# Row-max jobs in key-chunk order, and six of eight head groups in a hardware loop

## The reference

```
mod = silu(condition) @ Wada + bada          # 6 vectors: shift, scale, gate, twice
xm  = layernorm(x) * (1 + sc_a) + sh_a
q, k, v = xm @ Wqkv                          # 16 heads of 32
attn = softmax(causal(q @ k.T / sqrt(32)))
x   = x + gt_a * ((attn @ v) @ Wproj + bproj)
xm  = layernorm(x) * (1 + sc_m) + sh_m
x   = x + gt_m * (gelu(xm @ W1 + b1) @ W2 + b2)
```

## Time and profile before

| | |
|---|---|
| median of 3 runs | 2236.31 us (2230.17 to 2239.51) |
| the profiled execution's own time | 2236.31 us |
| its span | 2234.1 us |
| attention phase | 346 to 1391 us, and 8 us of its end |
| POOL busy in 346 to 1391 us | 861.07 us |
| DVE busy in it | 743.77 us |
| ACT busy in it | 631.35 us |

### The profile page before, as it was taken

How to read it: one execution, slowest core, us unless ns; L and a number is a source line. 1 busy time by engine, 2 the same in 40 slices (tenths; PEclk the granted TensorE clock), 3 DMA queues, 4 the chain that set the end, 5 groups by cost and what they waited for, 6 DMA issues and landing times. The chain is left out here.

```text
span 2234.1 us, 31272 instructions
## 1 busy us (share of the span) xinstructions
PE 2154.2 (96%) x11326; PEld 1443.9 (65%) x11326; DVE 1286.7 (58%) x2872; ACT 929.2 (42%) x1780; POOL 965.7 (43%) x380
## 2 busy tenths in 40 slices
PE   6999999999999999999999999899999999999998
PEld 5888885454444545454444544677888888888886
DVE  4778876777777777777777754784313213133132
ACT  2111115566566656655655665335322222222221
POOL 2001007979799797988979773760000000000000
PEclk9999999999999999999999999999999999999999
DMA  6548346235261522625243222784101011011010
GB/s 235 206 151 266 127 168 158 63 76 120 54 138 46 119 66 63 149 49 131 52 112 80 59 77 63 247 319 155 67 37 57 0 56 56 0 56 56 0 38 19
DMA packets 129240, 222.96 MB, mean 100 GB/s; under 512 B 8526, under 2 KB 26006, under 8 KB 128920
## 3 DMA queue, kind: packets, MB, share of 16 engines
q1 hardware_dynamic: 107992, 179.38, 29.5%
q10 hardware_dynamic: 21120, 41.95, 5.1%
HBM read 146.31 MB, written 74.98 MB: 99 GB/s over the span
## 5 line engine op out<-in xcount | busy, mean ns | idle before, releaser
L1170 ACT ACTIVATE prob<-st 128x512 f32<-128x512 f32 (+3 forms) x1280 | 608.0, 542 | 387.2 <-PE st L1344 371.6
L1140 POOL TENSOR_TENSOR psum_k<-psum_k,prob 128x2048 f32<-128x2048 f32 (+1 forms) x150 | 670.8, 4472 | 21.0 <-ACT prob L1170 5.4
L1226 DVE TENSOR_REDUCE part<-mx 128x1 f32<-128x512 f32 x702 | 459.0, 685 | 107.0 <-PE mx L1324 104.0
L1344 PE MATMUL st<-q_st,k_st 98*128 98x512 f32 (+3 forms) x1280 | 489.8, 395 | 8.1 <-ACT prob L1170 4.1
L1324 PE MATMUL mx<-k_st,qx_st 96*128 96x512 f32 (+3 forms) x1189 | 465.7, 407 | 17.7 <-DVE part L1222 5.6
L1738 DVE TENSOR_TENSOR m_g_lo<-m_g,m_g_hi 128x512 fp32r<-128x512 f32 x128 | 88.6, 693 | 494.8 <-ACT m_g_hi L1652 494.8
L1344 PEld LDWEIGHTS st<-q_st,k_st 98*128 98x128 f32 x1280 | 242.7, 190 | 194.3 <-issue 103.1
L1324 PEld LDWEIGHTS mx<-k_st,qx_st 96*128 96x128 f32 x1189 | 224.0, 190 | 169.7 <-DVE part L1226 107.3
L1222 DVE CUSTOM_DVE_ANT_0 unused<-mx,mask_row 128x256 bf16<-128x256 f32 x487 | 230.6, 485 | 124.8 <-PE mx L1324 119.7
L1361 PE MATMUL o_ps<-prob,v_sb 128*32 128x512 f32 (+3 forms) x2560 | 285.6, 551 | 3.0 <-POOL prob L1123 3.0
L1648 ACT ACTIVATE m_g<-m_hid,vcol 128x512 f32<-128x512 f32 x128 | 88.2, 689 | 480.3 <-PE m_hid L1835 480.3
(11 more groups left out here) (168 smaller groups left out, 2593.5 us busy)
## 6 DMA issues: line engine op xcount, KB each, us to landing
k_st<-qk_scratch SPq DMA_DIRECT2D x96, 256.0 KB, 8.3
qx_st<-qk_scratch SPq DMA_DIRECT2D x96, 256.0 KB, 5.0
q_st<-qk_scratch SPq DMA_DIRECT2D x96, 256.0 KB
qk_scratch<-st_hi ACTq DMA_DIRECT2D x16, 1024.0 KB, 4.2
qk_scratch<-st_lo ACTq DMA_DIRECT2D x16, 1024.0 KB, 6.9
xs<-in_x_dram SPq DMA_DIRECT2D x8, 1024.0 KB, 8.7
v_sb<-v_scratch SPq DMA_DIRECT2D x8, 1024.0 KB, 15.4
o_scratch<-o_sb SPq DMA_DIRECT2D x32, 256.0 KB, 2.3
```

Of the source, the lines that this page charges most:

```text
L1140: nc.gpsimd.tensor_tensor(dst, src, prob[:, s % BUF, :, m:], ALU.add).then_inc(pool_added, 1)
L1170: nc.scalar.activation(prob[:, s % BUF, h, m:], st[n % RING][:, m:], ACT.Exp, scale=SCALE).then_inc(exp_done, 1)
L1226: nc.vector.tensor_reduce(most, bank[:, 0:w], AX.X, ALU.max).then_inc(mx_free, 1)
L1344: nc.tensor.matmul(st[n % RING][:, m:], k_st[u][0:MROWS, h, kt * P:(kt + 1) * P], q_st[0:MROWS, pos % 2, h, m:], start=True, stop=True).th ...
```

## The change

Three edits, of which the third has the most instructions:

```
-                       for h in range(GH) for t in range(TT) for kc in range(c + 1)[::-1]]
+                       for kc in range(c + 1)[::-1] for h in range(GH) for t in range(TT)]
...
-            work.insert(start + LATER, (pos or QC) - 1)
+            work.insert(start + (LATER if pos else 0), (pos or QC) - 1)
...
-        rest = [it for it in self.items[len(self.tail):self.items.index(QC - 1) + 1]
-                if not self.norm(it) and (isinstance(it, int) or it[0])]
+        rest = [it for it in self.items[len(self.tail):self.items.index(QC - 1) + 1] if not self.norm(it)]
...
-            for g in range(NG):
-                body(g, g % 2, g > 0, g < NG - 1)
+            body(0, 0, False, True)
+            with eng.Fori(0, NG // 2 - 1) as i:
+                body(2 * i + 1, 1, True, True)
+                body(2 * i + 2, 0, True, True)
+            body(NG - 1, 1, True, False)
```

## The result

The changed kernel took 2259.93 us (median of 4 runs, 2256.48 to 2262.04) against 2236.32 us (4 runs). The ratio is 1.0113, 95% interval 1.0095 to 1.0132: about 1% slower. I had forecast 2241 us with a range of 2224 to 2264. The profiled execution of after took 2256.66 us, its span is 2254.9 us, 20.8 longer than before.

A forecast was written before the change was run, and what follows sets the result against it. Bound taken: POOL's additions in a chain POOL, ACT, POOL, with DVE nearly as close. Sum: 2236.31 + 2.8 (order) + 3.7 (clock) + 2.8 (turn) + 0.6 - 6.6 - 2 + 4 = 2241.6, rounded to 2241 us; range 2224 to 2264.

The forecast's parts named there:

- the slower rival: Whole kernel: jumps back stall PE, ACT and DVE, with turn delay and clock falls, giving 2261 us; chance 0.23.
- the account that I took as mine: Whole kernel: the forecast itself, 2241 us with its own range 2232 to 2250; chance 0.42.
- The jump back, 2 us, twice: At the loop's round end: PE idle 2 us each time, bounds 0.86 and 4.3 us; +4 us in all.
- PE has products queued at that place: At the loop's round end: queued matmuls on PE as the reason to take 2 us a jump, below 4.3.
- The waits in the loop, -8.6 us: Groups in the loop: POOL's pauses 0.1 us shorter each, -6.6 us; ACT's first exponentials gain too, -2 us.
- the bound of 0.9: First half of a loop group (pos 0): POOL's shorter pauses save no more than some 0.9 us.
- Registers at 0: Loop body in attention: 710 register instructions a round on PE and 462 on ACT, taken to cost 0 us.
- The order of the jobs, +2.8 us: Reordered blocks: changes up to block 13 hidden, +0.4 us in blocks 16 and 17, over 7 groups.
- The early turn, +0.4 us a group: Block 8, groups 0 to 6: last `st` waits for `mcol`, delaying POOL's addition; bounds 0 and 0.8; +2.8 us.
- The clock, +3.7 us: Block 17, now nearly all short jobs: two more falls to half clock; bounds 0 and 11 us.
- the sign I had set for myself: Groups 1 to 6 without a jump changing over 2 us each would mean registers or waits weigh more than given.
- Phase a, +0.6 us: Phase a: one job more, group 0's share growing from 29 to 30 items, one DVE operation of 0.6 us.

The follow-up runs named there:

- edits 1 to 3 alone: New job order and early turn of batch 3 against the kernel before, all groups written out without the hardware loop: 2249.32 us, ratio 1.0059.
- the loop alone: Hardware loop put on the old job order, against the kernel before: 2245.56 us, ratio 1.0046.
- Keys alone: Jobs ordered by key chunk instead of by head, against the kernel before; turn of batch 3 as before, no loop: 2241.72 us, ratio 1.0023.
- the turn alone: Turn of batch 3 moved early, against the kernel before; jobs by head as before, no loop: 2250.46 us, ratio 1.0076.
- the test with a delay: Last exponential of block 8 cut into four pieces in every group, against the kernel before: 2238.13 us, ratio 0.9994.
- the kernel that differs in group 0 alone: Four exponentials of step 17 cut into four pieces each, in group 0 only, against the kernel before: 2238.57 us, ratio 1.0003.

## Why the prediction was right or wrong

The result lies in the range, 19 us above the value. The range holds it thanks to the slower rival, to which I gave 0.23; the account that I took as mine would have left it out (2232 to 2250). Most of the miss, 15 of 19 us, is in the loop. My terms for it were -6.6, -2 and +4, so -4.6 us; alone it cost 0.46%, 10 us. The other terms together were +9.9 us; edits 1 to 3 alone cost 0.59%, 13 us, so 3 more.

- **The jump back, 2 us, twice: the step that failed.** It cost 4.38 and 4.30 us of PE's time, my upper bound (4.3), and the clock at half in the next block, which I had only in the rival. In the loop alone that is 5.8 and 6.2 us against before, 12 in all, 8 more than taken; in after the two blocks are 4.9 us longer each time, 9.7 in all. "PE has products queued at that place" hid nothing: the last of them start at 755.90 us and take 0.40, and PE stands still behind them. That a taken jump stops PE was right; the overlap was wrong, and the size was that of the slower rival.
- **The waits in the loop, -8.6 us.** POOL's pause shrank to 0.08 us, not 0.05, and a first part without a jump gained 0.6 us. That is the 9 pauses times 0.07 us: from POOL's first addition to the end of its last one of pos 0 it takes 52.0 to 52.1 us in the groups of the loop without a jump, and 52.6 before. All of it came through, so the bound of 0.9 that I had set never came into play. Pos 1 and ACT gave 0.2 us a group at most (the second parts of groups 2, 3 and 5 of the loop alone are 76.0 to 76.1 us, against 76.2 to 76.4 before, all behind a fall in block 7). For the two groups with a jump the gain is inside the price of the jump. So some 2.5 to 3.5 us, 5 to 6 fewer than taken.
- **Registers at 0: right.** Groups of the loop without a jump are shorter than before.
- **The order of the jobs, +2.8 us.** Keys alone cost 0.23%, 5 us. That POOL hides what blocks 2 to 6 gain in length was right, to 0.1 us. Wrong was "Are diagonal jobs in a row dearer than singly? ... so no": I compared with block 7, whose `st` are short. Under full `st`, 11 jobs in a block are dearer than their sum (block 10 +0.4, where I had -0.25; block 4 +0.5, where I had +0.15). Block 8, where I had nothing, grew by 0.5, and block 17 by 0.45 instead of 0.3. Blocks 2 and 13 came as computed (-0.2, -0.3), the latter though I had POOL letting nothing of it through.
- **The early turn, +0.4 us a group.** The mechanism was right, and in the turn alone POOL's idle time of 1.46 us is the 1.4 forecast; in after itself it is 2.3 to 3.8 us, and no run takes that apart. But I followed only the `st` behind the turn; the products wait too, and block 8 grew by 0.7, close to my bound of 0.8: +2 us.
- **The clock, +3.7 us.** Block 17 fell in seven groups, five more than before, and is 8.8 us longer over them. But the short jobs by themselves, as I had argued, don't do it: keys alone fell there in two groups, like before, and the turn alone in six with the old jobs. And the sign I had set for myself, groups without a jump over 2 us longer, did come in three of the four (group 4: 135.40 against 131.1; group 1 only 1.2), but did not mean what I had tied to it, registers or waits: the loop alone has first parts 0.6 us shorter there. It was the falls, the turn and the order.
- **Phase a, +0.6 us:** not seen; attention began at 345.0 us, against 346.8.

The rival "the loop's cost lies on the path" had 12 us for the jumps, 5.6 for the turn, 11 for falls, -4 for the waits. Measured: 12 in the loop alone and 9.7 in after, about 5, about 9 in block 17 of after, -2.5 to -3.5. It had no term for the order of the jobs, which cost 5 us alone, so that it came so near to 2260 is in part luck. But it was the better account, in its parts as well. The Trainium skill's rule on taken branches ("Runtime: NRT & Kernel Launch", Instruction fetch mechanics) spoke for it, and I underrated that. My own value rested on a cover, queued products, that I had not looked for in the rows at a group's end.

What stays open: what makes the clock fall in block 17 of one group and not of the next. That a turn with a wait in block 8 costs more than its own length is shown over the runs (0.32 and 0.76%, of which its own length explains some 0.1 and 0.2), and that the clock is lower with it too (0.982 and 0.979, against 0.985), but not by what path; the test with a delay was too small to tell. And that what stops PE at the jump is the fetch of its instructions is inferred: the packets are there, the wait for them is in no row.

## What to carry to other kernels

A jump back over a long body must be priced as PE standing still plus the half clock behind it, unless the trace shows work queued there; multiply by the taken jumps, not by the rounds. When an instruction that waits is moved earlier, count everything behind it on its engine, up to the end of the block, and not only the next one. And where the clock falls in other places from one execution to the next, trust the medians and the mean clocks over many runs, and take the falls of one profile as a sample.

## What the runs showed of the hardware

- The taken jump back over a body of 2920 PE instructions held PE for 4.0 to 4.4 us, seven times in four kernels; leaving the loop held it for 0.3 us at most (a block of 6.02 us beside 5.7). The block behind the jump ran at 0.60 to 0.74 of full clock and took 1.2 to 2.5 us more than in the loop's groups without a jump.
- POOL's pause between dependent additions depends on which instruction carries which wait: 0.15 us with both on the addition, 0.07 with the wait for the exponentials on an instruction of its own (37.64 and 37.18 us for eight additions, in two kernels that differ in this alone).
- TensorE's clock went to half in other groups from one profile to the next though those groups held the same instructions (blocks 7 and 17: six times in before, ten in the kernel that differs in group 0 alone), with the same median and the same mean clock over the runs.
